# Experts' inner values computed transposed, with the expert's up weights fetched tile by tile

## The reference, cut to what matters

```
xn  = layernorm(x)                               # 8192 tokens x 128
xr  = rms_norm(xn) * scale                       # ids = nearest of 8 centroids, per token
h   = xr @ up_w[e]                               # 128 -> 512: a = first 256, g = last 256
y   = (a * silu(g)) @ down_w[e]                  # 256 -> 128, e the token's expert
out = y + xn                                     # then x = x + s * silu(out), and layer one
```

## Time and profile before

| | |
|---|---|
| median of 3 runs | 1221.29 us (1216.65 to 1221.37) |
| the profiled execution | 1218.42 us, of which the span of the trace is 1216.7 us |
| PE, DVE, ACT, POOL busy, whole span | 88%, 79%, 72%, 65% |
| expert steps in the trace | about 170 to 390 us |
| layer one in the trace | 392 to 1216 us |

### The profile page before, as it was taken

The page is one execution under the profiler, slowest core; times in us unless marked ns, Lnnn a source line. Parts: engine busy times, 40 slices in busy tenths (PEclk is TensorE's granted clock), DMA queues, the critical chain, the costliest instruction groups (busy, mean ns, idle before and its releaser), DMA issues.

```text
span 1216.7 us, 29072 instructions
## 1 busy us (share of the span) xinstructions
PE 1068.0 (88%) x8602; PEld 682.5 (56%) x8603; DVE 959.5 (79%) x2148; ACT 880.9 (72%) x2187; POOL 791.2 (65%) x1147
## 2 busy tenths in 40 slices
PE   2766369999987589999999999999999999999985
PEld 1655246667764355555655565555655565555642
DVE  6678988888996477888788878888888887888861
ACT  2555338777765368888888888888888888888874
POOL 4476767666786266667766776677667766776630
PEclk9866679999998699999999999999999999999998
DMA  9611111111211332233323322332233223322310
GB/s 247 175 41 37 33 54 49 47 45 46 58 42 34 81 89 65 66 91 83 78 65 92 86 74 68 92 86 72 70 90 90 68 73 86 88 71 74 81 37 11
DMA packets 148166, 89.27 MB, mean 73 GB/s; under 512 B 73080, under 2 KB 137272, under 8 KB 147768
## 3 DMA queue, kind: packets, MB, share of 16 engines
q1 hardware_dynamic: 143928, 79.01, 25.4%
q0 software_dynamic: 4096, 8.53, 2.5%
HBM read 55.91 MB, written 31.47 MB: 72 GB/s over the span
## 4 chain that ended last, share of the span: by engine, by line
PE 51%; issue 6%; DVE 4%; ACT 4%; SPq 1%; DMA 1%; POOL 0%; DVEq 0%; POOLq 0%
PE PS L1943 8%; PE PS L1933 6%; PE PS L1919 5%; PE PS L2008 5%; PE PS L2030 5%; ACT PT L1793 3%; DVE bm L1583 3%; PE PS L2022 3%; PE PS L1995 3%; PE PS L1985 3%; PE PS L1957 3%; PE PS L1889 3%; PE PS L1973 3%; PE PS L2039 2%; PE PS L1897 1%
## 5 line engine op out<-in xcount | busy, mean ns | idle before, releaser
L1583 DVE TENSOR_REDUCE bm<-PS 128x16 f32<-128x1024 f32 x256 | 312.4, 1220 | 32.9 <-PE PS L1919 25.2
L1793 ACT ACTIVATE PT<-PS 128x1024 f32<-128x1024 f32 x256 | 262.5, 1025 | 22.2 <-PE PS L1933 18.6
L1943 PE MATMUL PS<-PT,rows 128*32 128x256 f32 x2048 | 137.9, 387 | 1.7 <-ACT OT L1798 1.7
L1472 POOL TENSOR_TENSOR Pr<-Pr,linv 128x512 f32<-128x512 f32 x128 | 131.9, 1042 | 5.0
L1767 ACT ACTIVATE Pr<-PS,nmf 128x256 f32<-128x256 f32 x256 | 117.5, 475 | 0.0
L1933 PE MATMUL PS<-QS,KS 51*128 51x256 bf16 x1024 | 100.0, 273 | 13.6 <-ACT PT L1793 8.4
L1603 DVE TENSOR_REDUCE nmf<-PS 128x4 f32<-128x1024 f32 x64 | 78.4, 1225 | 42.4 <-PE PS L2008 42.4
L1919 PE MATMUL PS<-KS,QS 48*128 48x256 bf16 x1024 | 101.3, 276 | 10.1 <-DVE bm L1583 6.0
L476 POOL DMA_INDIRECT xs_dram<-rows,slot x64 | 66.1, 1032 | 40.3 <-DVEq L704 22.6
L1011 PE MATMUL PS<-S,wmix 128*128 128x256 f32 (+1 forms) x192 | 70.2, 452 | 16.8 <-DVE diff L732 16.3
L1985 PE MATMUL PS<-xT,wsel 128*128 128x256 f32 x256 | 74.6, 416 | 8.6 <-DMA wsel<-in_qkv_w 7.8
(11 more groups left out here) (258 smaller groups left out, 2830.6 us busy)
## 6 DMA issues: line engine op xcount, KB each, us to landing
wsel<-in_qkv_w SPq DMA_DIRECT2D x128, 96.0 KB
parts_dram<-parts SPq DMA_DIRECT2D x32, 384.0 KB
QS<-parts_dram SPq DMA_DIRECT2D x64, 96.0 KB
KS<-parts_dram SPq DMA_DIRECT2D x64, 96.0 KB
xs_dram<-zero_t SPq DMA_DIRECT2D x1, 4752.0 KB, 27.2
xs_t<-xs_dram SPq DMA_DIRECT2D x72, 66.0 KB, 1.8
ys_dram<-ys_t SPq DMA_DIRECT2D x72, 64.0 KB, 1.6
QS<-parts_dram SPq DMA_DIRECT2D x64, 64.0 KB
```

The lines of the kernel that those rows point to most:

```text
L1472: pool.tensor_tensor(Pr[i][:, qt, :, :], Pr[i][:, qt, :, :], linv[:, i, qt, :].unsqueeze(2).broadcast_to([P, 2, SEQ]), ALU.mult).then_inc( ...
L1583: dve.tensor_reduce(bm[:, i // 2, :, 2 * (i % 2):2 * (i % 2) + 2, :].rearrange("p q r b -> p r q b"), bS.rearrange("p (r q b k) -> p r q b ...
L1793: act.activation(PT[i % 4][:, :, :], bT.rearrange("p (r k) -> p r k", r=2), ACT.Exp).then_inc(s_exp, 1)
L1943: last = pe.matmul(bC[j * VC:(j + 1) * VC, 0:SEQ], V2[q][:, kt, 4 * g + j, :], PT[(2 * g + j // 2) % 4][:, j % 2, kt * SEQ:(kt + 1) * SEQ] ...
```

## The change

The up product is computed transposed: the expert's up weights become the stationary operand, in four blocks of 128 columns, and the tokens the moving one, so that `psU` holds the hidden values with the hidden index on the partitions. `hid` then goes into the down product as it is; its transposition on PE and the copy on ACT are gone. The factors of the normalization, which used to be applied behind the products by a scale per token, are now applied ahead: ACT scales the tile's rows (`xsr`) before PE transposes them, and applies the per-feature scale in the copy to `xsT`. `psX` has two banks. The up weights are no longer kept: SP reads the tile's expert from `tile_expert` into a register and fetches its 256 KB into one of four `up` buffers, once per tile. The hardware loop is written out as steps. The gathers of the first two batches are spread over steps 20 to 31, with `first_rows` now in two halves. In layer one the minus-one rows are written per batch, behind `load_qk` of batches 0 to 3, and the last batch's shifted scores alternate between `bT` and `bS`.

The stages of turn n are now: `load` n + 3, `load_up` n + 1, `xsr` n, transposition and `xsT` n - 1, up product and tanh n - 2, gate products n - 3, down product and `ys_t` n - 4, `skip` n - 5, `store` n - 6.

```diff
-        up = sb("up", [P, NE * 2 * HID])
+        up = [sb(f"up{i}", [P, 2 * HID]) for i in range(NUP)]
...
-        gate, hid, hidT = ([work[:, (3 * k + i) * HID:(3 * k + i + 1) * HID] for i in range(3)] for k in range(3))
+        gate, hid, xsr = ([work[:, (3 * k + i) * HID:(3 * k + i + 1) * HID] for i in range(3)] for k in range(3))
...
-            for s in range(first, STATIC):
-                step(s // NQ, s % NQ)
-            with eng.Fori(STATIC // NQ, TAIL // NQ) as quad:
-                for p in range(NQ):
-                    step(quad, p)
-            for s in range(TAIL, END + 3):
+            for s in range(first, END + 3):
                 step(s // NQ, s % NQ)
...
-            sp.dma_start(up[:, :], up_w).then_inc(s_we, 16)
...
             def load(t, h, q):
-                after(sp, s_fx, t - 2)
+                after(sp, s_xsr, t - 2)
...
+            def load_up(t, h, q):
+                after(sp, s_up, t - NUP + 1)
+                sp.load(expert_registers[q % TPS], tile_expert[0:1, bass.ds(t, 1)])
+                e = sp.snap(expert_registers[q % TPS], min_val=0, max_val=NE - 1)
+                apart(sp)
+                sp.dma_start(up[q % NUP][:, :], up_w[:, bass.ds(e * 2 * HID, 2 * HID)]).then_inc(s_upl[q % NUP], 16)
...
                     new = tile(quad, p, turn, -3)
                     if new and (not isinstance(new[0], int) or new[0] >= 3):
                         load(*new)
+                    soon = tile(quad, p, turn, -1)
+                    if soon and (not isinstance(soon[0], int) or soon[0] >= 1):
+                        load_up(*soon)
                     done = tile(quad, p, turn, LAST)
...
             def experts(quad, p, turn):                              # ACT
-                now = tile(quad, p, turn, 0)
+                now = tile(quad, p, turn, 1)
...
-                    act.copy(xsT[q % 3][:, :], psX[:, 0:P]).then_inc(s_xsT, 1)
-                now = tile(quad, p, turn, 3)
-                if now:
-                    t, h, q = now
-                    act.wait_ge(s_fh, t + 1)
-                    after(act, s_dn, t - 2)
-                    act.copy(hidT[q % 3], psH[:, 0:2 * P]).then_inc(s_hidT, 1)
+                    act.activation(xsT[q % 3][:, :], psX[q % 2][:, 0:P], ACT.Identity, scale=scale_c[:, 0:1]).then_inc(s_xsT, 1)
                 now = tile(quad, p, turn, 4)
...
-                    act.activation(ys_t[q % 3][:, :], psY[:, 0:D], ACT.Identity, scale=xs_t[q][:, D + 1:D + 2]).then_inc(s_y, 1)
-                now = tile(quad, p, turn, 1)
+                    act.activation(ys_t[q % 3][:, :], psY[:, 0:D], ACT.Identity, scale=0.5).then_inc(s_y, 1)
+                now = tile(quad, p, turn, 0)
+                if now:
+                    t, h, q = now
+                    act.wait_ge(s_xs[q % 3], arrivals(h, q))
+                    after(act, s_fx, t - 2)
+                    act.activation(xsr[q % 3][:, 0:D], xs_t[q][:, 0:D], ACT.Identity, scale=xs_t[q][:, D:D + 1]).then_inc(s_xsr, 1)
+                now = tile(quad, p, turn, 2)
...
-                    pe.matmul(psU[q % 2][:, :], xsT[q % 3][:, :], up[:, bass.ds(e * 2 * HID, 2 * HID)],
-                              start=True, stop=True).then_inc(s_up, 1)
+                    for c in range(2 * HID // P):
+                        last = pe.matmul(psU[q % 2][:, c * P:(c + 1) * P], up[q % NUP][:, c * P:(c + 1) * P], xsT[q % 3][:, :],
+                                         start=True, stop=True)
+                    last.then_inc(s_up, 1)
...
-            for i in range(NQ):
+            def load_minus_rows(i):
...
                     load_qk(*batch1)
+                    if batch1[0] < NQ:
+                        load_minus_rows(batch1[0])
```

More of the change, by code:

```diff
@@ L181, in layer_zero @@
         TPS = 3
+        NUP = 4
         G = NQ * TPS
@@ L291, in layer_zero @@
         s_tab = sem("tile_table_ready")
-        s_ups = sem("up_scaled")
+        s_upl = [sem(f"up_loaded{i}") for i in range(NUP)]
         s_xs = [sem(f"xs_loaded{i}") for i in range(3)]
+        s_xsr = sem("xs_scaled")
         s_fx = sem("xs_transposed")
@@ L518, in constants, with first_rows @@
                     pool.tensor_copy(first.identb[:, :], ident[:, :])
[L520 to L527, removed]
+            def first_rows(t, j):
+                if j == 0:
+                    pool.tensor_copy(first.slot_t[t][:, :], slot[:, t * TB:t * TB + TB]).then_inc(first.s_slot, 1)
+                    pool.wait_ge(first.s_slot, t + 1)
+                    for i in range(3):
+                        pool.wait_ge(s_ys[i], 16 * (OPEN // 3))
+                pool.indirect_dma_start(first.Y[t][:, j, :], None, ys_dram[0:OPEN * P, :],
+                                        bass.IndirectOffsetOnAxis(first.slot_t[t][:, j:j + 1], axis=0)).then_inc(first.s_y[t], 16)
             def first_residual(t):
@@ L756, in experts @@
             def experts(quad, p, turn):
-                now = tile(quad, p, turn, 2)
+                now = tile(quad, p, turn, 3)
                 if now:
@@ L841, in step @@
                     denominator(*m)
[L842 to L845, removed]
+                for t in range(NFIRST):
+                    if s == TAKE + 3 * t + 4:
+                        first_gated(t)
+                    if s == TAKE + 3 * t + 6:
+                        first_stats(t)
             run(dve, step)
@@ L916, in experts @@
                     after(act, s_hid, t - 2)
-                    act.activation(gate[q % 3][:, :], psU[q % 2][:, HID:], ACT.Tanh, scale=xs_t[q][:, D:D + 1]).then_inc(s_gate, 1)
+                    act.activation(gate[q % 3][:, :], psU[q % 2][:, HID:], ACT.Tanh, scale=0.5).then_inc(s_gate, 1)
             def scalings(k):
@@ L969, in step @@
                     scalings(s - FIRST - 2)
-                if s in (TAKE + 1, TAKE + 2):
-                    first_tanh(s - TAKE - 1)
+                for t in range(NFIRST):
+                    if s == TAKE + 3 * t + 3:
+                        first_tanh(t)
                 take(3)
-                if s == B // NQ:
-                    act.wait_ge(s_we, 32)
-                    act.activation(up[:, :], up[:, :], ACT.Identity, scale=scale_c[:, 0:1]).then_inc(s_ups, 1)
             run(act, step)
@@ L1034, in transposes @@
             def transposes(quad, p, turn):
-                now = tile(quad, p, turn, 0)
+                now = tile(quad, p, turn, 1)
                 if now:
                     t, h, q = now
[L1038 to L1048, removed]
+                    pe.wait_ge(s_xsr, t + 1)
+                    after(pe, s_xsT, t - 1)
+                    pe.transpose(psX[q % 2][:, 0:P], xsr[q % 3][:, 0:D], ident[:, :]).then_inc(s_fx, 1)
             def products(quad, p, turn):
@@ L1054, in products @@
                     e = pe.snap(experts_of[q], min_val=0, max_val=NE - 1)
-                    pe.wait_ge(s_hidT, t + 1)
+                    pe.wait_ge(s_hid, t + 1)
                     after(pe, s_y, t)
                     for c in range(2):
-                        last = pe.matmul(psY[:, 0:D], hidT[q % 3][:, c * P:(c + 1) * P], down[:, bass.ds(e * 2 * D + c * D, D)],
+                        last = pe.matmul(psY[:, 0:D], hid[q % 3][:, c * P:(c + 1) * P], down[:, bass.ds(e * 2 * D + c * D, D)],
                                          start=(c == 0), stop=(c == 1))
@@ L1193, in layer_one @@
         o_t = two("o_t", [P, TB, D])
-        s_neg = sem("minus_one_rows_loaded")
+        s_neg = [sem(f"minus_one_rows_loaded{i}") for i in range(NQ)]
         s_slot = first.s_slot
@@ L1275, in layer_one, with shifted_bank @@
         bF, bR = (bF1, bF2), (bS, bT)
+        def shifted_bank(t, i):
+            return bS if t == B - 1 and i % 2 == 1 else bT
         def v_bank(t):
```

78 lines of the change are left out of this document (42 added, 36 removed).

## The result

The changed kernel takes 1328.42 us (median of 4 runs, 1324.75 to 1329.79) against 1221.33 us for the kernel before beside it: a ratio of 1.0873, 95% interval 1.0844 to 1.0903, so 107 us more. The profiled execution has a span of 1327.6 us, 110.9 more than before.

A forecast was written before the change was run, and what follows sets the result against it. PE was taken to bound the kernel before; a new loop through SP and memory would set 4.93 us per turn. The profiled 1218.4 + 124.5 (63 turns) - 3 (layer one's start) - 4 (last batch) = 1336 us, range 1268 to 1398.

The forecast's parts named there:

- What bounds the kernel before: Expert steps: PE is the bound, its output projection setting 8.86 us per step; DVE next at 7.69.
- the ring: Expert steps: from one `xsr` to the next lies one full round through SP and memory; no turn can be shorter.
- Its price: One round: 0.14 + 0.42 + 0.90 + 0.47 + 2.4 + 0.6 = 4.93 us per turn, ends 3.9 and 5.93.
- the register load: SP's read of the tile's expert: 0.71 us, at least 0.48; with the transfer's issue 0.90 us of the round.
- Landing: Store behind the 256 KB of up weights lands 2.4 us after its issue, ends 1.6 and 3.4.
- Rivals 2 and 3: Store lands 1.6 us after issue, not queued: 1285 us, 17%; lands after 3.4, as behind `in_l_w`: 1399 us, 10%.
- The sum for the 63 turns: Turns 7 to 69 take 310.6 us instead of 186.1: +124.5 us, low +59.6, high +187.5.
- that stall: Step 20: gathers wait for a store of turn 29, holding POOL's queue; taken as 0, up to 5 us without cover.
- rival 4: Expert steps: PE at 1.2 GHz becomes a second bound, 1 us more per step over 21 steps, 1357 us, 13%.
- The sign that PE's busy share would fall to about half: Expert steps: PE has some 7.4 us of work per 14.8 us, at a clock under 1.
- The seams: Layer one: -3 us at its start (ends -3.9, +2), -4 us in the last batch (ends -2, -5).
- rival 1: Expert steps: the loop isn't binding, DVE sets 7.69 us per step, worth 25 us; 1186 us in all, 5%.

The follow-up runs named there:

- store first: The changed kernel with SP issuing the store first in each turn, then the token load, then the up weights: 1192.12 us, ratio 0.9853 to the kernel before.
- the fourth buffer: The changed kernel with four buffers for `ys_t` in place of three, SP's order kept: 1196.19 us, ratio 0.9883 to the kernel before.
- The small transfer: The changed kernel with each up transfer cut from 256 KB to 16 KB, register load kept: 1275.78 us, ratio 1.0519 to the kernel before.
- store first with the gathers from step 22: The changed kernel with SP's store first and the first two batches' gathers begun at step 22, not 20: 1199.07 us, ratio 0.9825.
- the first four kernels of the experiments: Changed kernel with store first, four `ys_t` buffers, no register load, or small up transfer: 1192.12, 1196.19, 1306.60, 1275.78 us; kernel before beside them 1211.9.
- the last three: Kernel before with layer-one parts alone, or loop written out; changed kernel with store first and gathers from step 22: 1212.88, 1219.72, 1199.07 us.

## Why the prediction was right, step by step

The prediction was 1336 us, in a range of 1268 to 1398; the median is 1328.4.

- **What bounds the kernel before**: PE, which the traces bear out. With only the loop written out, PE is busy 19.95 of 20 us at 8.36 us per step; with the ring gone and less work for PE (store first), steps fall to 8.0 to 8.1 us, and DVE is busy 19.35 of 20 us and PE 19.17. No run takes work from PE and changes nothing else.
- **The ring**: shown from both ends, by SP's order and by the fourth buffer, and in the trace by one whole round.
- **Its price**: forecast 4.93 us per turn, measured 4.62 in an undisturbed round and 4.82 on average. The terms: wake-up of SP 0.14 as forecast; `load` to `load_up` 0.89, forecast 0.42 + 0.90 = 1.32; to the store 0.44 (0.47); landing and wake-up 2.58 (2.4 + 0.05); `ys_t` and `xsr` on ACT 0.57 (0.55). The mis-sized term is the register load: I took 0.71 us from a load of four values, and this one reads one value in 0.27. The total came nearer than its terms, by luck: 63 undisturbed rounds of 4.62 us would be 19.5 us less than forecast, and 12.6 us of that came back in turns that took longer, which I had not costed. Of 61 turns timed from `load` to `load`, 20 took 4.78 us or more; in most of these it was the store that landed later, 2.7 to 3.6 us from its issue to ACT's write, where the median is 2.59. Landing was the term with the widest ends, 1.6 to 3.4; the value between, by transfer time, came within 0.1 us of the measured 2.5. The small transfer shows that the queue ahead makes the difference, 2.5 against 1.6. Rivals 2 and 3, which differ in this term alone and put it at 1.6 and 3.4, are refuted by the measured 2.5.
- The rule of the Trainium skill in "DMA: Bandwidth & Descriptors", section "Queues, rings and completion order", that a semaphore follows all earlier writes of its DMA engine, agrees: on the medians a store lands 0.44 + 2.5 = 2.94 us after the issue of the up weights ahead of it, which land after 2.8. That a store can't land before the up weights ahead of it, as I worked out from the rule, also needs both to run on the same DMA engines; no view here shows that.
- **The sum for the 63 turns**: forecast +124.5, measured +117.6, in which there are some 3.6 us of the gather's stall at step 20. In that round SP's store stands 3.67 us behind `load_up` in place of 0.45, since POOL's `skip` of its tile stood behind the gather. I had costed that stall at nothing, with up to 5 us without cover: the cover, idle time in a long turn, was not enough for 13.7 us of POOL's waiting. The steps before step 13 took 2.4 us less than before.
- **PE's clock** (rival 4): the granted clock was 0.87 in the stretch above, so mostly 2.4 GHz, and PE's idle time ended with ACT. It was no second bound. The sign that PE's busy share would fall to about half failed: it was 27.27 of 40 us, 68%, or 9.9 us per step of 14.46 where I had 7.4. As the Trainium skill has it in "TensorE: Matmul & The Clock Gate", Part 1, less activity goes with a lower clock; the trace agrees, with 1.00 at 19.62 of 20 us busy before and 0.87 at 27.27 of 40 us now. Here that cost nothing that can be seen.
- **The seams**: forecast -3 and -4. The start of layer one gave 3.6 us, the last batch 3.9 (72.7 us from its first matmul to the end, 76.6 before), and alone on the kernel before both together 6.6 us by the time. The reason I gave for the last batch holds for the larger part only. Its eight exponentials start over 9.1 us, where I had 7.8 and where it was 11.8 before, which is 2.7 of the 3.9 us; the first and the last of them in the changed kernel:

```profile
1306.08 1.02 ACT L1802 ACTIVATE PT<-PS 128x1024 f32<-128x1024 f32 x1 [0.32 <-PE PS L1946]
...
1315.17 1.02 ACT L1802 ACTIVATE PT<-PS 128x1024 f32<-128x1024 f32 x1
```

- **The faster case** (rival 1) was not this kernel's, and its price was too high: with the ring out of the way the time is 16 to 23 us under that of before (four buffers, store first, store first with the gathers from step 22), where I had 32. The term that failed is the pace of 7.69 us in the steps, put at 25 us: nearly all steps take 8.0 to 8.6, and the 21 steps give 14.7 us at best (186.1 to 171.4). DVE's reciprocals are 7.69 us apart in single steps only.

## What to carry to other kernels

When a wait at the head of an in-order queue is moved to another engine, draw the ring: what that engine itself waits for, and whether it stands in the same queue behind the new wait. The price of a turn is then the whole round, register load, issues and landing, and busy shares show nothing of it beforehand. A store whose buffer is soon needed belongs ahead of loads that have time, or needs one buffer more.

## What the runs showed that I had not expected

- A register load on SP took 0.27 us for one value (72 of them) and 0.71 us for four.
- A transfer's landing depends on what was issued shortly ahead of it in the same queue: 64 KB of outputs landed after 1.6 us behind 16 KB, 2.5 us behind 256 KB, and 2.7 us when that was itself issued closer behind 66 KB.
- Most of layer one runs at different speeds from chip to chip. From its fifth batch's first matmul to its last batch's it took 653.9 us in the kernel before and 657.1 in the changed one. It took 644.1 to 648.6 us in the first four kernels of the experiments and 653.4 to 655.0 in the last three, one execution of each. So most of the spread, some 10 us, goes with the chip, as the medians of the kernel before do, 1211.9 and 1221.9 us. Among the first four it was 648.6 and 648.1 in the two that have the ring and 644.1 and 644.5 in the two that don't; the cause of that difference is open. It is why the ratios are taken on one chip, and why single microseconds of a whole time are not assigned to an edit here.
